# Two-way attention: VectorE's statistics, context parts, difference and norm placed behind the turned weights, and x turned ahead of the mix

## What is computed

```python
Q_char = _linear(char_emb, Wq_c, bq_c)      # char_emb is x
K_sub = _linear(subword_emb, Wk_s, bk_s)    # subword_emb is ctx_1024
V_sub = _linear(subword_emb, Wv_s, bv_s)
scores = jnp.einsum('bqh,bkh->bqk', Q_char, K_sub) * scale
char2sub = jnp.einsum('bqk,bkh->bqh', jax.nn.softmax(scores, axis=-1), V_sub)
Q_sub = _linear(subword_emb, Wq_s, bq_s)
K_char = _linear(char_emb, Wk_c, bk_c)
V_char = _linear(char_emb, Wv_c, bv_c)
scores2 = jnp.einsum('bqh,bkh->bqk', Q_sub, K_char) * scale
sub2char = jnp.einsum('bqk,bkh->bqh', jax.nn.softmax(scores2, axis=-1), V_char)
gate_in = jnp.concatenate([char2sub, sub2char], axis=-1)
gate = jax.nn.sigmoid(jnp.einsum('blh,oh->blo', gate_in, Wg) + bg)
return gate * char2sub + (1 - gate) * sub2char
...
x = _layernorm(x + _L0_xattn_ref(x, ctx_1024, ...), axis=-1)
```

## Time and profile before

| | us |
|---|---|
| median of 3 runs (lowest, highest) | 2001.73 (1990.87, 2002.68) |
| profiled execution, its time | 2008.87 |
| profiled execution, its span | 2007.5 |
| TensorE busy in the span | 1674.5 (83%) |
| VectorE, ScalarE, GpSimd busy | 1149.6, 1011.2, 983.3 |

### The profile page before, as it was taken

The page is one execution under the profiler, slowest core; times in us unless marked ns, Lnnn a source line. Parts: engine busy times, 40 slices in busy tenths (PEclk is TensorE's granted clock), DMA queues, the critical chain, the costliest instruction groups (busy, mean ns, idle before and its releaser), DMA issues. The chain is left out here.

```text
span 2007.5 us, 23647 instructions
## 1 busy us (share of the span) xinstructions
PE 1674.5 (83%) x7418; PEld 1222.8 (61%) x7419; DVE 1149.6 (57%) x2237; ACT 1011.2 (50%) x1933; POOL 983.3 (49%) x832
## 2 busy tenths in 40 slices
PE   5698896699972798989996999989999997589992
PEld 2476675587761465656764666656656665566661
DVE  4665655566645676767745665665575573542223
ACT  2154442455521376766774776666676673142222
POOL 1200000344324266676882775675585584058885
PEclk9899998799996599999998999999999998679996
DMA  2300100544424332222102110121020120248777
GB/s 82 128 12 0 32 22 21 186 109 114 121 45 124 81 82 65 72 64 74 43 21 87 28 44 22 33 62 25 25 67 25 25 60 22 62 98 193 183 181 172
DMA packets 96785, 146.15 MB, mean 73 GB/s; under 512 B 22711, under 2 KB 61820, under 8 KB 93830
## 3 DMA queue, kind: packets, MB, share of 16 engines
q1 hardware_dynamic: 66448, 104.92, 18.1%
q0 software_dynamic: 18432, 26.36, 7.5%
q10 hardware_dynamic: 11782, 13.37, 2.2%
HBM read 101.83 MB, written 36.41 MB: 69 GB/s over the span
## 5 line engine op out<-in xcount | busy, mean ns | idle before, releaser
L2261 POOL TENSOR_TENSOR STp_lo_use<-ST_use,STp_hi_use 128x512 fp32r<-128x512 f32 x256 | 337.7, 1328 | 202.2 <-ACT ST_use L2091 200.9
L1737 POOL TENSOR_TENSOR STp_lo<-ST,STp_hi 128x512 fp32r<-128x512 f32 x192 | 248.2, 1313 | 106.1 <-ACT ST L1512 104.7
L2156 DVE TENSOR_REDUCE nmax_use<-bank 128x1 f32<-128x512 f32 x256 | 173.4, 679 | 111.7 <-PE bank L1996 107.2
L2087 ACT ACTIVATE STp_hi_use<-bank 128x512 fp32r<-128x512 f32 x256 | 152.9, 597 | 163.1 <-PE bank L2022 159.3
L1630 DVE TENSOR_REDUCE nmax<-bank 128x1 f32<-128x512 f32 x256 | 170.9, 683 | 53.8 <-PE bank L1426 53.1
L1426 PE MATMUL bank<-rows_k,rows_q 65*128 65x512 f32 x256 | 135.9, 539 | 38.3 <-DVE nmax L1630 20.5
L2091 ACT ACTIVATE ST_use<-bank 128x512 f32<-128x512 f32 x256 | 151.8, 593 | 2.0 <-POOL STp_lo_use L2261 2.0
L1509 ACT ACTIVATE STp_hi<-bank 128x512 fp32r<-128x512 f32 x192 | 117.0, 609 | 58.0 <-PE bank L1437 57.6
L924 POOL TENSOR_SCALAR veps<-mv 128x4 f32<-128x4 f32 x4 | 0.9, 228 | 253.1 <-DVE mv L873 253.1
L1996 PE MATMUL bank<-ks,qs 128*128 128x512 f32 x256 | 110.5, 432 | 10.2 <-DMA ks<-ks 9.6
L1512 ACT ACTIVATE ST<-bank 128x512 f32<-128x512 f32 x192 | 118.2, 616 | 0.0
(11 more groups left out here) (443 smaller groups left out, 4644.5 us busy)
## 6 DMA issues: line engine op xcount, KB each, us to landing
stage<-in_W SPq DMA_DIRECT2D x16, 1024.0 KB, 4.9
Wgu<-in_Wgu SPq DMA_DIRECT2D x32, 384.0 KB, 3.4
rows_q<-hop_scratch SPq DMA_DIRECT2D x32, 256.0 KB, 4.3
ks<-ks SPq DMA_DIRECT2D x64, 128.0 KB, 2.3
rinv<-rinv_scratch SPq DMA_DIRECT2D x64, 128.0 KB, 2.9
rows_k<-hop_scratch SPq DMA_DIRECT2D x24, 256.0 KB, 5.3
hop_scratch<-qkp_hi SPq DMA_DIRECT2D x20, 256.0 KB
Wda<-in_Wdn SPq DMA_DIRECT2D x32, 128.0 KB, 3.8
```

Source lines behind the costliest of these rows:

```text
L1737: G.tensor_tensor(parts_of(u)[1], ST[u % TB], plain(parts_of(u)[0]), ALU.subtract).then_inc(low.sem, low.inc(u))
L2087: A.activation(STp[u % NHI][0], bk.ap, ACT.Exp)
L2156: V.tensor_reduce(nmax[:, (h % 2) * TB + j:(h % 2) * TB + j + 1], bk.ap, AX.X, ALU.max, negate=True).then_inc(bk.free, 1)
L2261: G.tensor_tensor(STp[u % NHI][1], ST[u % NFULL], plain(STp[u % NHI][0]), ALU.subtract).then_inc(low["pool"].sem, low["pool"].inc(u))
```

## The change

Nothing is added to or taken from the work; every engine issues the same instructions in another order, and `norm` is split into `add_turned` (sum with x) and `average` (statistics).

- Turned weights of direction 1, key tile 0: ahead of the last value projection of the next batch, on TensorE, ScalarE and VectorE.
- x of the next batch is turned ahead of the mix.
- The context's parts leave `take_source` and stand ahead of the fourth exponent (ScalarE) and the fourth peak (VectorE) of direction 1, as `take_context`.
- VectorE: the difference stands behind two peaks of direction 0; the sum with x behind two peaks of direction 1, the statistics at the end of the iteration; turned weights ahead of the scaling that stood before them; the norm's last step in the next iteration, behind the turned weights. ScalarE: each turned weight one exponent sooner.

```diff
@@ -565,6 +565,7 @@
         att_low = Signal(kit, "s2_att_low", [(k, d) for k in range(B) for d in range(2)])
         mixed = Signal(kit, "s2_mixed", range(B))
         Q_BANK, K_BANKS, O_BANKS, S_BANKS = 7, (3, 4), (5, 6), (0, 1, 2)
+        FIRST_TURN_BEFORE = "V", 1, 0
 
         def s_bank(k, d, j):
             return bank[S_BANKS[((2 * k + d) * TB + j) % 3]]
@@ -603,6 +604,8 @@
                     PE.wait_ge(bk.free, bk.free_at["x", k])
                 PE.wait_ge(ctx_low.sem, ctx_low[k])
                 for what, c, bk in projections(d):
+                    if k and (what, c, d) == FIRST_TURN_BEFORE:
+                        turn_prob(k - 1, 1, 0)
                     n = bk.use((what, k, d, c))
                     if n:
                         PE.wait_ge(bk.free, n)
@@ -674,8 +677,9 @@
             for k in range(B + 1):
                 if k < B:
                     project(k, 0)
+                if k == B:
+                    turn_prob(k - 1, 1, 0)
                 if k:
-                    turn_prob(k - 1, 1, 0)
                     turn_prob(k - 1, 1, 1)
                     weigh(k - 1, 1, 0)
                     turn_prob(k - 1, 1, 2)
@@ -690,10 +694,10 @@
                     gates(k - 1)
                 if k < B:
                     project(k, 1)
+                if k + 1 < B:
+                    turn(k + 1)
                 if k:
                     turn_mix(k - 1)
-                if k + 1 < B:
-                    turn(k + 1)
                 if k < B:
                     score(k, 1, 0)
                     score(k, 1, 1)
@@ -716,12 +720,15 @@
                     bk = bank[(Q_BANK, K_BANKS[0])[c]]
                     A.wait_ge(bk.full, bk.full_at["x", k])
                     A.activation(xp[0][:, c, :], bk.ap, ACT.Copy).then_inc(src_high.sem, src_high.inc((k, "x%d" % c)))
-                if k:
-                    A.wait_ge(ctx_in.sem, ctx_in[k])
-                    A.activation(ctxp[0], ctxT, ACT.Copy).then_inc(ctx_high.sem, ctx_high.inc(k))
+
+            def take_context(k):
+                A.wait_ge(ctx_in.sem, ctx_in[k])
+                A.activation(ctxp[0], ctxT, ACT.Copy).then_inc(ctx_high.sem, ctx_high.inc(k))
 
             def take_projections(k, d):
                 for what, c, bk in projections(d):
+                    if k and (what, c, d) == FIRST_TURN_BEFORE:
+                        take_turned(k - 1, 1, 0)
                     A.wait_ge(bk.full, bk.full_at[what, k, d, c])
                     if what == "V":
                         m = A.activation(Vp[d][0][:, 2 * c:2 * c + 2, :].rearrange("p t d -> p (t d)"), bk.ap, ACT.Copy)
@@ -768,7 +775,7 @@
                 if k < B:
                     take_projections(k, 0)
                 if k:
-                    for kt in range(TB):
+                    for kt in range(0 if k == B else 1, TB):
                         take_turned(k - 1, 1, kt)
                     take_out(k - 1, 1)
                 if k < B:
@@ -782,10 +789,12 @@
                     take_source(k + 1)
                 if k < B:
                     exponent(k, 1, 0)
+                    take_turned(k, 0, 0)
                     exponent(k, 1, 1)
-                    take_turned(k, 0, 0)
+                    take_turned(k, 0, 1)
                     exponent(k, 1, 2)
-                    take_turned(k, 0, 1)
+                    if k + 1 < B:
+                        take_context(k + 1)
                     exponent(k, 1, 3)
                     take_turned(k, 0, 2)
                     take_turned(k, 0, 3)
@@ -803,12 +812,15 @@
                     bk = bank[(Q_BANK, K_BANKS[0])[c]]
                     V.wait_ge(src_high.sem, src_high[k, "x%d" % c])
                     V.tensor_tensor(xp[1][:, c, :], bk.ap, plain(xp[0][:, c, :]), ALU.subtract).then_inc(bk.free, 1)
-                if k:
-                    V.wait_ge(ctx_high.sem, ctx_high[k])
-                    V.tensor_tensor(ctxp[1], ctxT, plain(ctxp[0]), ALU.subtract).then_inc(ctx_low.sem, ctx_low.inc(k))
+
+            def take_context(k):
+                V.wait_ge(ctx_high.sem, ctx_high[k])
+                V.tensor_tensor(ctxp[1], ctxT, plain(ctxp[0]), ALU.subtract).then_inc(ctx_low.sem, ctx_low.inc(k))
 
             def take_projections(k, d):
                 for what, c, bk in projections(d):
+                    if k and (what, c, d) == FIRST_TURN_BEFORE:
+                        take_turned(k - 1, 1, 0)
                     V.wait_ge(high.sem, high[what, k, d, c])
                     if what == "V":
                         hi, lo = (v[:, 2 * c:2 * c + 2, :].rearrange("p t d -> p (t d)") for v in Vp[d])
@@ -838,11 +850,12 @@
             def take_out(k, d):
                 V.wait_ge(att_out.sem, att_out[k, d, DC - 1])
                 V.tensor_tensor(cTp[1][:, DC * d:DC * d + DC, :], cT[:, DC * d:DC * d + DC, :], plain(cTp[0][:, DC * d:DC * d + DC, :]), ALU.subtract).then_inc(att_low.sem, att_low.inc((k, d)))
-                if d:
-                    if k:
-                        obk = bank[O_BANKS[1]]
-                        V.wait_ge(obk.full, obk.full_at["M", k - 1])
-                    V.tensor_tensor(mix, cT[:, 0:DC, :], cT[:, DC:2 * DC, :], ALU.subtract).then_inc(own.sem, own.inc(("difference", k)))
+
+            def difference(k):
+                if k:
+                    obk = bank[O_BANKS[1]]
+                    V.wait_ge(obk.full, obk.full_at["M", k - 1])
+                V.tensor_tensor(mix, cT[:, 0:DC, :], cT[:, DC:2 * DC, :], ALU.subtract).then_inc(own.sem, own.inc(("difference", k)))
 
             def blend(k):
                 for c in range(DC):
@@ -855,7 +868,7 @@
                 V.wait_ge(own.sem, own["twice", k])
                 V.scalar_tensor_tensor(mix, mix, 0.5, cT[:, DC:2 * DC, :], ALU.mult, ALU.add).then_inc(mixed.sem, mixed.inc(k))
 
-            def norm(k):
+            def add_turned(k):
                 for t in range(TB):
                     bk = bank[O_BANKS[t // 2]]
                     if t % 2 == 0:
@@ -863,6 +876,8 @@
                     m = V.tensor_tensor(summed[:, t, :], bk.ap[:, (t % 2) * D:(t % 2 + 1) * D], X[:, k * TB + t, :], ALU.add)
                     if t % 2:
                         m.then_inc(bk.free, 1)
+
+            def average(k):
                 for t in range(TB):
                     if t % 2 == 0:
                         V.wait_ge(bank[O_BANKS[t // 2]].free, bank[O_BANKS[t // 2]].free_at["M", k])
@@ -884,12 +899,19 @@
                 if k < B:
                     take_projections(k, 0)
                 if k:
-                    for kt in range(TB):
+                    for kt in range(0 if k == B else 1, TB):
                         take_turned(k - 1, 1, kt)
+                    if k > 1:
+                        normed(k - 2)
                     take_out(k - 1, 1)
                 if k < B:
                     find_peak(k, 0, 0)
-                    for j in range(1, TB):
+                    find_peak(k, 0, 1)
+                if k:
+                    difference(k - 1)
+                if k < B:
+                    over_sum(k, 0, 0)
+                    for j in range(2, TB):
                         find_peak(k, 0, j)
                         over_sum(k, 0, j - 1)
                     over_sum(k, 0, TB - 1)
@@ -899,24 +921,29 @@
                     take_projections(k, 1)
                 if k + 1 < B:
                     take_source(k + 1)
-                if k:
-                    norm(k - 1)
                 if k < B:
                     find_peak(k, 1, 0)
                     find_peak(k, 1, 1)
+                if k:
+                    add_turned(k - 1)
+                if k < B:
+                    take_turned(k, 0, 0)
                     over_sum(k, 1, 0)
-                    take_turned(k, 0, 0)
                     find_peak(k, 1, 2)
+                    take_turned(k, 0, 1)
                     over_sum(k, 1, 1)
-                    take_turned(k, 0, 1)
+                    if k + 1 < B:
+                        take_context(k + 1)
                     find_peak(k, 1, 3)
                     over_sum(k, 1, 2)
                     take_turned(k, 0, 2)
                     take_turned(k, 0, 3)
                     over_sum(k, 1, 3)
+                if k:
+                    average(k - 1)
+                if k < B:
                     take_out(k, 0)
-                if k:
-                    normed(k - 1)
+            normed(B - 1)
 
         def pool():
             for k in range(B):
```

## The result

The changed kernel takes 1975.32 us in the median of 4 runs (1969.87 to 1980.55), the kernel before 1998.76 us beside it (4 runs); the ratio is 0.9895, 95% interval 0.9865 to 0.9924. 1980.4 us was forecast from a median of 2001.73, a ratio of 0.9894.

What follows compares the result with a forecast made beforehand. TensorE was taken as the bound, with idle time and low clock to win. Iterations 0 to 4 save 0.7 + 7.2 + 9.2 + 2.9 + 1.3 = 21.3 us: 2001.73 - 21.3 = 1980.4 us, range 1970 to 1992.

Steps and rivals of the forecast that it cites:

- steps of the sum: Step times read from the trace before, such as 2.77 us from peak start to TensorE, used to time the new order.
- Part 1: Turned weights ahead of the last value projection cover the 1.14 us pause before weighing: 1.0 us a batch saved.
- the late value part: Value projection's low part, freeing the bank for the weighing's second half, comes 0.2 us late.
- Part 2: Difference behind two peaks: about 0.5 us left of the 1.55 us pause at the fourth score, 1.1 us a batch saved.
- Part 3: x turned ahead of the mix: the 0.97 us pause shrinks to 0.2, scores begin at 176.9 and not 177.7.
- Part 4: Statistics, context and x's sum behind iteration 1's peaks: 4.22 us pause becomes 0.7; with part 3, 5.1 us saved.
- the new pause: At the third weighing, 1.8 us, because the fourth peak stands behind the context's low part on VectorE.
- (a): Rival: the clock falls at the new pauses in iterations 0 to 2, costing 5 to 9 us, 1985 to 1989; chance 0.18.
- (b): Rival: the low clock lasts after the three falls; at 20 us each 30 us lost, 2010; chance 0.03.
- (c): Rival: VectorE, not TensorE, sets the pace in the scores' half; 4 to 9 us less gain, 1984 to 1989; chance 0.12.
- (d): Rival: ScalarE really sets the pauses, the peaks' move buys nothing, 15 of 21 us fail, 1996; chance 0.05.

Runs made afterwards that it cites:

- the norm's move alone: Kernel before with only the norm split and moved (sum with x behind two peaks, statistics at iteration's end, last step next iteration): iterations 1 and 2 57.15 and 57.17 us.
- the experiment on the difference: Changed kernel with the difference put back ahead of the two peaks of direction 0: iterations 1 and 2 take 55.18 and 55.22 us.

## Why the prediction was right

The steps of the sum held, and the largest differences between forecast and measurement have opposite signs. By iteration, forecast and measured from the first pair of traces: iteration 1, 7.2 and 61.31 - 54.08 = 7.2; iteration 2, 9.2 and 63.29 - 54.07 = 9.2, where a second trace of the kernel before, with a shorter low clock, gives 8.1; iteration 0, 0.7 and, from its first score, 30.03 - 29.32 = 0.7; iterations 3 and 4 up to the weighing at 322.40, 4.2 and (322.40 - 260.80) - (302.65 - 245.72) = 4.7, in which the sum with x, counted at nothing, has its part: the pause ahead of iteration 3's first weighing goes from 0.81 to 0.44 us. In all 21.3 forecast, 20.7 as the mean of two traces each, and 21 us (1.05%) in the ratio. That the total is so close is in part luck: iteration 2's 9.2 leant on a trace in which the low clock lasted 1.1 us longer than in the second one, and iteration 3 was put 0.5 too low. So is the nearness of 1980.4 to 1975.32: the base of 2001.73 was 3 us above the median of 1998.76 that the result stands beside.

*Part 1*: 1.0 forecast, 0.9 by undoing it; the late value part shows 0.17 us (0.2 forecast). *Part 2*: 1.1 forecast, 1.1 by undoing it, the pause 0.41 us (0.5). *Part 3*: in iteration 1 the scores of direction 1 begin 38.65 us in (176.22 - 137.57) and not 41.52 (177.72 - 136.20); less the 2.0 us won before the fourth score, that is 0.9 (0.8 forecast), and no pause is left of the 0.97 (0.2 forecast). Alone, in the kernel before, the move is worth 2.0 us, which the part did not say. *Part 4*: the weighing pauses 0.44 us (0.7) and the new pause is 1.52 us (1.8), 0.3 us sooner both; the fourth peak stands behind the context as forecast. Parts 3 and 4 together give 7.2 - 2.0 = 5.2 us (5.1). The peaks were held by the list, as the norm's move alone shows. What the part did not see is that the new pause need not be: with the context left where it was, an iteration takes 0.95 us less.

Two moves were not tried by themselves: the turned weights ahead of the scaling on VectorE, and each of them one exponent sooner on ScalarE. In iteration 1 the moves that were tried one at a time come to 4.2 (norm) + 2.0 (x) + 0.9 + 1.1 - 0.95 (context) = 7.25 us, against 7.2 for the whole change. That leaves nothing for those two if the moves simply add, and no run shows that they do.

*Rivals.* (a) The clock does not fall at the new pauses: with pauses of 0.41 to 1.52 us it is 1.00 over all of iterations 1 and 2 (windows above). The rule of the Trainium skill (TensorE: Matmul & The Clock Gate, A second HAM failure mode: psum-queue depth-cycling) on small idles that make the clock swing did not show here; the page's case is in bf16, this one is not. The rows of the kernel before spoke a little less against (a) than the prediction has it: its stage also has a pause of 3.07 us, at the gate (334.81), with a clock of 0.71 in the 5 us behind it, so the shortest pause with a fall was 3.07 and not 4.09. (b) falls with (a). (c) VectorE does hold back one thing, the fourth peak, but the pause that it leaves is 1.52 us, where 1.8 was forecast, and not one step longer. (d) falls with the norm's move, which touches VectorE's list alone and takes 2.6 us off the pause of 4.22, and with the experiment on the difference: moving a VectorE instruction moved the pause that the profile puts down to ScalarE.

What the forecast is least sure of is its base and not its sum: between the two profiled executions of the kernel before, the span moves by 11.6 us, more than half of the gain.

## What to carry to other kernels

Where engines have written-out lists, write down for each pause which instruction ended it, and then what stood ahead of that instruction in its own engine's list; work that nobody waits for (statistics, the norm's last step, a difference) belongs behind it. Steps of one chain, read from an undisturbed place in the same trace, gave the new order's pauses to 0.3 us. When a part is moved off one chain, look which chain it lands on: the context's parts cost 1 us an iteration in their new place, and an idle slot of 0.94 us had opened at the old one.

A short pause is also filled from the other side, by work of the waiting engine that needs nothing of the late one: the fourth score, and half of the gate's matmuls, filled theirs.

## What the runs showed of the hardware

In this stage none of the 33 pauses of TensorE of 1.25 to 1.67 us, in twelve traces, was followed by a lower clock: the 5 us behind each are at 1.00. Behind pauses of 2.80 to 3.10 us, from iteration 1 up to the gate, it fell in some executions and not in others: behind 2.80 us in 7 of 8, behind 3.10 in 1 of 2, behind the gate's 3.07 in 7 of 11. The changed kernel has the same code and the same pause of 3.07 us at the gate in both its traces, and the clock behind it is 1.00 in the first (window 314.30 above) and 0.66 in the second. Behind the seven pauses of 4.09 to 4.27 us it fell every time.

A TensorE that is busy with small matmuls can stay at 1.2 GHz. In the router's stretch of the last stage (matmuls with 32 columns and transposes) the kernel before ran at 0.50 for 16 us in which TensorE was never idle. In the changed kernel's second trace the 16 us from the same point of the same code ran at 0.85 on average, and TensorE got through 98 instructions and not 78. The window of that stretch in the kernel before:

```profile
1721.00:1737.00 16.00, 16.00 (x78) 16.00 (x78) 7.45 (x45) 1.38 (x3) 0.00 (x0) 0.50 0.22 75
```

and in the changed kernel's second trace:

```profile
1692.00:1708.00 16.00, 12.96 (x98) 11.51 (x97) 11.17 (x63) 2.05 (x4) 0.00 (x0) 0.85 0.22 75
```

From the router's first matmul to the first expert's it takes 58.6 us in the one and 51.2 in the other. The twelve traces take either 50.8 to 51.2 us (six of them) or 58.2 to 58.6 (six): the kernel before both times the longer (58.6, 58.4), the changed kernel the longer and then the shorter (58.3, 51.2). That is 7 us of the scatter between runs, a third of what this change gains. The DMA share is the same in both windows and the clock is not; what sets the clock there, no run shows.
